# A two-pass graph network on one core: a fifth early group, row slots released by the reading product, half of the first stored unit summed between the passes

## The chip, the cores and the metric

The kernel runs on one core of one Trainium2 chip. The metric is device time in microseconds (us). Before the change it is 1505.38 us, the median of three runs (1504.96, 1505.38 and 1505.86). One further execution was recorded by the hardware profiler, and all rows below come from it.

## The reference

There are N = 6250 nodes with 96 features and E = 100000 edges, sorted by destination, each with 32 edge features and a weight. Two layers follow each other.

```
# layer 0: gated messages
e   = concat(x[src], edge_attr)
msg = (gelu(e @ mW1 + mb1) @ mW2 + mb2) * sigmoid(gelu(e @ gW1 + gb1) @ gW2 + gb2)
agg = segment_sum(msg, dst)
h   = layernorm(x + gelu(concat(x, agg) @ uW1 + ub1) @ uW2 + ub2) * ln_g + ln_b
x1  = layernorm(x + h)
# layer 1: graph convolution with self loops; deg and dinv come from the weights
out = segment_sum((x1 @ W)[src] * dinv[src] * weight * dinv[dst], dst) + self loop + b
x2  = layernorm(x1 + out)
```

## The kernel before, in words

Edges lie in 98 groups of 8 tiles of 128 edges, nodes in 49 blocks of 128. The kernel makes two passes over the groups.

**First pass** (layer 0). GpSimd (POOL) gathers the rows x[src] of each group with 8 indirect DMAs, TensorE (PE) transposes them and multiplies by the weights, ScalarE (ACT) applies gelu, VectorE (DVE) gates the messages, and PE sums them into windows of 72 nodes. Beside it, blocks of nodes that have all their messages are finished by `block1_sums` and `block1_rows` on DVE: the scaled node rows x1·dinv (`x_nat`, counted by the semaphore `s_xs`) go to a table in HBM, `x1s_table`.

**Second pass** (layer 1). It needs, for each edge, the scaled row of its source node. Half of the groups are *dense* (list `DENSE`, 48 of them): during the first pass a matrix of cells, one per group, was built and stored in HBM (`b_table`, 2 MB a unit). In the second pass SyncE (SP) loads a unit in two halves into one of three buffers, and PE multiplies it by all 49 blocks of `x_nat` (`dense_sums`, line 741). The other 50 groups are *gathered* (list `GATHERED`): POOL fetches their rows from `x1s_table`, 8 indirect DMAs a group, into one of 8 slots `rows`, DVE makes their one-hot matrix, and PE multiplies both (`gathered_sums`, line 823). Gathered groups are called G0 to G49 here, in the order in which POOL fetches them.

The second pass is written out in 26 *turns* (0 to 25). Turns 0, 1, 24 and 25 have one dense unit, the others two; `TAKES` says how many gathered groups each turn takes. Within a turn PE runs chunks 0 to 31 of the dense sum, with the turning over and placing of the turn before in between (`turn_over`, `place_sums`), then the gathered products, then output products of blocks that became whole (`outputs`, line 795), then chunks 32 to 48. DVE adds the sums of a turn into `acc1` after the next turn's `place_sums` (line 1444, semaphore `s_acc2`); the first gathered product of a turn waits for the additions of the turn before. Products in `ps_win` are counted by `s_win3`, in the order of PE.

**Between the passes.** PE finishes the last node blocks (`end1`, line 716), DVE normalises them in two batches of four (line 1343), PE transposes each batch (`turned_blocks`, line 766), ACT and SP write the rows to `x1s_table`. Four groups, 3, 5, 7 and 9, are *early* (`EARLY`, fetched first as G0 to G3): POOL fetches their rows from a second table, `x1s_early`, that holds the first 39 node blocks only (line 519), before `x1s_table` is whole. The part of those groups that comes from the last 10 blocks is computed on PE from cells made by DVE (`early_hots`) at the end of turns 1 and 3, two groups each: `early_cells` (line 834, 16 products a group that ACT copies out), `early_sums` (line 842), `early_placed` (line 851).

POOL reuses a row slot when the group eight places before it has been added to `acc1`:

```
if i >= SLOTS:
    pool.wait_ge(s_acc2, PLACE[GATHERED[i - SLOTS]] + 1)
```

Nothing is scheduled by the hardware or by a planner: each engine runs its own list, in the order written, and semaphores join them.

Of the kernel before, what the change touches and what calls it, by code (L numbers as in the profile page):

```python
# [5 lines left out]
P = 128  # L6
N, E = 6250, 100000
ND, ED = 96, 32
TG = 8
# [6 lines left out]
W = 72  # L16
# [13 lines left out]
TW = TG * WD  # L30
EARLY = (3, 5, 7, 9)
RUNS = ((0, 1), (10, 1), (12, 7), (20, 3), (24, 1), (26, 1), (28, 1), (30, 1), (32, 1), (34, 1), (36, 1),
        (39, 2), (42, 1), (44, 1), (46, 1), (48, 1), (50, 1), (52, 1), (54, 1), (57, 1), (59, 2), (62, 1),
        (64, 1), (66, 1), (68, 1), (70, 1), (72, 1), (74, 1), (76, 1), (78, 1), (80, 1), (82, 1), (86, 1),
        (88, 1), (90, 3), (94, 1))
DENSE = [g for first, n in RUNS for g in range(first, first + n)]
# [16 lines left out]
CELLS = 2 * HW  # L53
EARLY_IN = {1: (0, 1), 3: (2, 3)}
EARLY_TURN = list(EARLY_IN)
TAKES = (0, 1, 4) + 21 * (2,) + (1, 2)
HOTS = 6
# [35 lines left out]
assert len(DENSE) * TG == 2 * TWOS and sum(PAIRS) == len(DENSE) and not set(EARLY) & set(DENSE)  # L93
assert all(b - a == 2 for a, b in zip(EARLY, EARLY[1:]))
assert all(a + b <= HOTS for a, b in zip(TAKES, TAKES[1:]))
# [4 lines left out]
def gnn_kernel(nc, t, out):  # L100
# [11 lines left out]
    with ctx:  # L112
# [18 lines left out]
        win_off = sb("win_off", [P, NW])  # L131
        due_i = sb("due_i", [P, 1], i32)
        due = sb("due", [P, 1])
        mats = sb("mats", [P, HC + 5 * ND + 1])
# [14 lines left out]
        lo = sb("lo", [NG, 1])  # L149
        hi = sb("hi", [NG, 1])  # L150
        reach = sb("reach", [NG, 1])
        crossed = shared[0:NG, 4400:4400 + NW]
        extra = sb("extra", [NG, 1])
        spread = shared[0:NG, 2860:2860 + 3 * NG + 1]
# [14 lines left out]
        spare = x1b[:, :, :].rearrange("p b c -> p (b c)")  # L169
        win_i = spare[:, 5 * NT + 2 * NG + HC:5 * NT + 2 * NG + HC + NW].bitcast(i32)  # L170
        before, lo_all = [spare[:, 5 * NT + NG * i:5 * NT + NG * (i + 1)] for i in range(2)]
        b1_hi = spare[0:3, 5 * NT + 2 * NG:5 * NT + 2 * NG + HC].bitcast(bf16).rearrange("p (k c) -> p k c", k=2)
# [49 lines left out]
        hot_node = spare_g[:, 2 * ND:2 * (ND + W)].rearrange("p (m w) -> p m w", m=2)  # L222
        early_rows = spare_2[:, 0:NE * ND].rearrange("p (e c) -> p e c", e=NE)
        early_node = spare_c[:, 0:NE * W].rearrange("p (e w) -> p e w", e=NE)
# [291 lines left out]
        def _(pool):  # L516
# [50 lines left out]
            with pool.If(hard < 1):  # L567
                pool.wait_ge(s_zeroed, 16)
                pool.wait_ge(s_early, 16 * DONE_B)
                for i in range(NE):  # L570
                    pool.wait_ge(s_xt, NG - SLOTS + i + 1)
                    early_gathers(i)
                pool.wait_ge(s_xt, NG)
                pool.wait_ge(s_xsw, 16 * NB)
                for i, g in enumerate(GATHERED):
                    if i >= SLOTS:
                        pool.wait_ge(s_acc2, PLACE[GATHERED[i - SLOTS]] + 1)
                    if i == len(GATHERED) - 1:
# [12 lines left out]
        def _(pe):  # L591
# [139 lines left out]
            def dense_sums(q, chunks):  # L731
                if q == 0 and chunks[0] == 0:
                    pe.wait_ge(s_xs, NB - LAST)
                    pe.wait_ge(s_tile_out, TWOS)
                if chunks[0] == 0:
                    wait(pe, s_rowsumc, q - 1)
                for c in chunks:
                    if c % HH == 0:
                        for d in UNITS[q]:
                            pe.wait_ge(s_loaded[d % NU][c // HH], 16 * (d // NU + 1))  # L740
                    mm = nc.tensor.matmul(raw_sums(q), x_nat[:, c, :], stored_cells(q, c), start=(c == 0), stop=(c == NB - 1))  # L741
                    if c == HH - 1:
# [103 lines left out]
            def early_placed(q, es):  # L846
                pe.wait_ge(s_early_rows, early_part_of[es[0]] + 1)
                pe.wait_ge(s_early_node, 1)
                for m, e in enumerate(es):
                    col = len(TURNS2[q]) + m  # L850
                    nc.tensor.matmul(ps_win[0:ND, W * col:W * (col + 1)], early_rows[:, e, :], early_node[:, e, :],
                                     start=True, stop=True)
# [41 lines left out]
        def _(act):  # L894
# [116 lines left out]
            def early_part(es):  # L1011
                for e in es:
                    act.wait_ge(s_early_cells, 2 * e + 2)
                    wait(act, s_early_sums, e - 1)
                    for m in range(2):
# [4 lines left out]
                act.wait_ge(s_early_sums, es[-1] + 1)  # L1020
                nc.scalar.activation(early_rows[:, es[0]:es[-1] + 1, :],
                                     ps_hid[0][0:TW, 0:2 * ND].rearrange("p (e c) -> p e c", c=ND),
                                     ACT.Copy).then_inc(s_early_rows, 1)
# [14 lines left out]
        def _(dve):  # L1038
# [89 lines left out]
            dve.wait_ge(s_bcast8, 1)  # L1128
            of_early = lambda a: a[:, TG * EARLY[0]:TG * (EARLY[0] + 2 * NE)].rearrange("p (e s) -> p e s", s=2 * TG)[:, :, 0:TG]
# [11 lines left out]
            nc.vector.tensor_copy(src_early[:, :].rearrange("p (e k) -> p e k", k=TG), of_early(low8))  # L1141
# [3 lines left out]
            nc.vector.tensor_scalar(cell_early[:, :].rearrange("p (e k) -> p e k", k=TG),  # L1145
                                    of_early(cell[:, :, 0:1].rearrange("p t o -> p (t o)")), float(-DONE_B * WD), None, ALU.add).then_inc(s_bcast8, 1)

# [387 lines left out]
```

## Time and profile before

| | |
|---|---|
| median of three runs | 1505.38 us |
| profiled execution, its own time | 1507.1 us |
| span of its trace | 1505.3 us |
| mean granted TensorE clock | 0.984 |
| PE busy | 1397.7 us (93%) |
| DVE busy | 1087.5 us (72%) |
| POOL busy | 1119.1 us (74%) |
| ACT busy | 536.7 us (36%) |
| DMA | 283.06 MB, mean 188 GB/s |

Times in the rows are microseconds from the start of the span. The first pass ends at about 1008 us, turn 0 begins at about 1023 us. A row of the time sequence says when a group of instructions started, how long it lasted, how many there were (a float32 product is recorded as two), and in brackets how long the engine had been idle before it and what released it. Matmuls overlap a little, so from start to start is the better measure of what a group costs. POOL's busy time leaves out about 0.30 us of issue between two gathers.

### The profile page before, as it was taken

How to read it: one execution, taken by the hardware profiler on the slowest of the kernel's cores; microseconds unless marked ns; L12 is line 12 of the kernel's file. 1: busy time of each engine (PE TensorE's matmuls, PEld its weight loads, DVE VectorE, ACT ScalarE, POOL GpSimd, SP SyncE). 2: the span in 40 equal slices, each digit the busy share in tenths (PEclk: the TensorE clock that was granted, in tenths of full speed). 3: DMA queues.
4: the chain of work that ended last, by engine and by line, in shares of the span. 5: the costliest groups of instructions: out<-in, count | busy, mean ns of one | idle time of the engine just before them, and what ended most of it. 6: DMA issues, size and time to landing. Idle time of an engine off the chain costs nothing.

```text
span 1505.3 us, 27016 instructions
## 1 busy us (share of the span) xinstructions
PE 1397.7 (93%) x9260; PEld 1156.5 (77%) x9261; DVE 1087.5 (72%) x2883; ACT 536.7 (36%) x835; POOL 1119.1 (74%) x1192
## 2 busy tenths in 40 slices
PE   3899999999999999999999999987999999999887
PEld 2677777777777777777777677767999999998887
DVE  7688899989999988888899888867434343334234
ACT  1355555555555555555555555540000000000000
POOL 7777777777777777777777777775777777777774
PEclk9899999999999999999999999988999999999999
DMA  3455555555565556555655565557567877777772
GB/s 100 135 151 151 176 169 168 154 173 165 168 174 180 155 152 187 155 156 162 187 168 156 153 183 168 153 182 261 204 209 280 289 264 276 263 266 262 261 239 64
DMA packets 137992, 283.06 MB, mean 188 GB/s; under 512 B 53235, under 2 KB 102387, under 8 KB 137852
## 3 DMA queue, kind: packets, MB, share of 16 engines
q1 hardware_dynamic: 88860, 208.35, 38.3%
q0 software_dynamic: 37760, 58.07, 17.5%
q10 hardware_dynamic: 11232, 14.85, 3.4%
q8 instruction: 77, 1.26, 0.3%
q14 instruction: 63, 0.52, 0.1%
HBM read 176.08 MB, written 105.09 MB: 187 GB/s over the span
## 4 chain that ended last, share of the span: by engine, by line
PE 72%; POOL 7%; DMA 5%; DVE 4%; issue 4%; ACT 3%; DVEq 2%; SPq 0%; ACTq 0%
PE ps_hid L662 15%; PE ps_hid L685 11%; PE ps_xt L685 10%; PE ps_xt L741 10%; PE ps_win L605 9%; POOL rows L534 7%; PE ps_xt L632 5%; DMA large<-b_table 4%; PE ps_hid L659 4%; PE ps_win L823 3%; ACT large L913 3%; PE ps_bt L702 1%; DVE shared L1250 1%; PE ps_bn L716 1%; PE ps_bn L795 1%
## 5 line engine op out<-in xcount | busy, mean ns | idle before, releaser
L534 POOL DMA_INDIRECT rows<-in_x_nat,idx x782 | 741.5, 948 | 238.4 <-issue 238.0
L534 POOL DMA_INDIRECT rows<-x1s_table,idx x360 | 339.7, 944 | 118.5 <-issue 109.1
L741 PE MATMUL ps_xt<-large,x_nat 128*96 128x160 f32 (+1 forms) x2548 | 350.9, 293 | 12.8 <-DMA large<-b_table 12.8
L741 PEld LDWEIGHTS ps_xt<-large,x_nat 128*96 128x96 f32 x2548 | 333.5, 163 | 16.2 <-DMA large<-b_table 9.4
L662 PE MATMUL ps_hid<-mats,large 128*128 128x192 f32 x1568 | 321.2, 328 | 0.0
L662 PEld LDWEIGHTS ps_hid<-mats,large 128*128 128x128 f32 x1568 | 268.3, 191 | 44.2 <-issue 31.6
L913 ACT ACTIVATE large<-ps_hid 128x768 f32<-128x768 f32 x196 | 158.9, 811 | 165.2 <-PE ps_hid L662 165.2
L1250 DVE TENSOR_TENSOR shared<-cell,ps_fix 128x2000 f32<-128x2000 f32 x96 | 213.7, 2226 | 0.0
L685 PE MATMUL ps_hid<-shared 128*128 128x500 f32 x384 | 184.0, 601 | 22.5 <-ACT large L913 22.5
L685 PE MATMUL ps_xt<-shared 128*128 128x500 f32 x384 | 179.8, 591 | 6.0 <-DVE shared L1250 6.0
L953 ACT ACTIVATE shared<-ps_hid 128x1000 f32<-128x1000 f32 x96 | 96.4, 1005 | 198.3 <-PE ps_hid L685 198.3
L605 PEld LDWEIGHTS ps_win<-hot,large 128*98 128x98 f32 x1568 | 144.9, 167 | 18.3 <-issue 15.3
L605 PE MATMUL ps_win<-hot,large 128*98 128x72 f32 x1568 | 152.4, 250 | 5.5 <-DVE acc L1170 3.6
L1009 ACT ACTIVATE shared<-ps_xt 96x160 f32<-96x160 f32 (+1 forms) x26 | 7.5, 289 | 404.5 <-PE ps_xt L741 404.5
L659 PE MATMUL ps_hid<-b_split,ones_b 128*128 128x384 bf16 x392 | 128.8, 329 | 5.7 <-DVE step L1115 4.0
L1256 DVE TENSOR_SCALAR shared<-ps_fix,dst_i,weight 128x128 f32<-128x128 f32 x384 | 130.4, 401 | 2.0 <-PE ps_hid L685 2.0
L953 ACT ACTIVATE shared<-ps_xt 128x1000 f32<-128x1000 f32 x96 | 96.4, 1004 | 87.5 <-PE ps_xt L685 78.9
L685 PEld LDWEIGHTS ps_xt<-shared 128*128 128x128 f32 x384 | 69.8, 192 | 73.3 <-issue 67.0
L685 PEld LDWEIGHTS ps_hid<-shared 128*128 128x128 f32 x384 | 65.3, 190 | 76.9 <-issue 44.0
L632 PE MATMUL ps_xt<-ident,rows 128*96 128x128 f32 x784 | 103.5, 276 | 12.3 <-DMA rows<-in_x_nat,idx 6.7
L897 ACT ACTIVATE large<-ps_xt 96x1024 f32<-96x1024 f32 x98 | 99.9, 1019 | 36.0 <-PE ps_xt L632 30.3
L1444 DVE TENSOR_TENSOR acc<-acc,ps_win 96x72 f32 x97 | 21.9, 226 | 121.2 <-PE ps_win L810 105.9
(177 smaller groups left out, 1471.6 us busy)
## 6 DMA issues: line engine op xcount, KB each, us to landing
b_table<-shared SPq DMA_DIRECT2D x192, 500.0 KB
large<-b_table SPq DMA_DIRECT2D x96, 1000.0 KB, 5.2
rows<-in_x_nat,idx POOLq DMA_INDIRECT x782
large<-in_edge_t ACTq DMA_DIRECT2D x96, 128.0 KB
rows<-x1s_table,idx POOLq DMA_INDIRECT x366, 2.9
large<-in_x_t SPq DMA_DIRECT2D x7, 336.0 KB
x_nat<-in_x_nat SPq DMA_DIRECT2D x7, 336.0 KB
out_nodes<-shared SPq DMA_DIRECT2D x46, 48.0 KB
```

Source lines behind the costliest of these rows:

```text
L534: nc.gpsimd.indirect_dma_start(out=rows[slot][:, k, :], out_offset=None, in_=table, in_offset=bass.IndirectOffsetOnAxis(ap=idx[:, TG * g + ...
L605: mm = nc.tensor.matmul(ps_win[0:rws, 0:W], lhs[:, k, :], hot[u][:, k, :], start=(k == 0), stop=(k == TG - 1))
L632: mm = nc.tensor.transpose(ps_xt[m // 4][0:ND, P * (m % 4):P * (m % 4 + 1)], rows[v][:, m, :], ident[:, :])
L659: nc.tensor.matmul(ps_hid[j][:, 0:2 * HC], ones_b[:, :], flat(b1_split[:, :, :]), start=True, stop=False)
L662: mm = nc.tensor.matmul(ps_hid[j][:, HC * q:HC * (q + 1)], feat[u][:, P * m:P * (m + 1)], w1[:, :], start=False, stop=(q == 1))
L685: mm = nc.tensor.matmul(ps_pair[pair][:, m, 0:CELLS], ring_low[:, r, :], flat(ring_place[:, 2 * r:2 * r + 2, :]), start=True, stop=True)
L741: mm = nc.tensor.matmul(raw_sums(q), x_nat[:, c, :], stored_cells(q, c), start=(c == 0), stop=(c == NB - 1))
L897: nc.scalar.activation(feat[u][0:ND, :].rearrange("p (m c) -> p m c", m=2), ps_pair[0][0:ND, :, :], ACT.Copy).then_inc(s_feat, 1)
L913: nc.scalar.activation(flat(hid[u][:, 4 * half:4 * half + 4, :]).rearrange("p (j c) -> p j c", j=2), ps_pair[1][:, :, 0:2 * HC], ACT.Gelu) ...
L953: nc.scalar.activation(ready_b[i % READY].rearrange("p (h m x) -> p m h x", h=2, m=2), ps_pair[pair][:, :, 0:CELLS].rearrange("p m (h x) - ...
L1250: return nc.vector.tensor_tensor(place, cells.to_broadcast(shape), places_ps.rearrange("p (o w) -> p o w", o=1).to_broadcast(shape), ALU.i ...
L1256: nc.vector.tensor_scalar(low[:, i, :], places_ps[:, 0:P], src_low[:, t0 + k:t0 + k + 1], weight[:, t0 + k:t0 + k + 1], ALU.is_equal, ALU. ...
```

## The change

There are four edits.

1. `EARLY` gets a fifth group, 12, which was dense; group 27, which was gathered, becomes dense in its place. There are still 48 dense and 50 gathered groups. POOL fetches 40 instead of 32 times from `x1s_early`, and 358 instead of 366 times from `x1s_table`. The late part of the fifth group is computed alone, at the end of turn 5; its sum uses one of the two places of `early_rows` again.
2. POOL's wait before it reuses a slot is on `s_win3` (PE has read the rows) instead of `s_acc2` (DVE has added the sums).
3. The first 25 of the 49 chunks of turn 0 stand before the transposes of the last eight blocks instead of behind the first four of them.
4. Turn 2 takes three gathered groups instead of four, turn 23 one instead of two, turn 24 two instead of one, turn 25 three instead of two. All other turns take two as before, so from turn 3 to turn 22 each has used one group less than before.

Beside these, several small tiles move into shared memory, and twelve small DVE instructions come to the start of the program, since five early groups at uneven distance are copied one by one. Cut to what matters:

```
-EARLY = (3, 5, 7, 9)
+EARLY = (3, 5, 7, 9, 12)
-EARLY_IN = {1: (0, 1), 3: (2, 3)}
+EARLY_IN = {1: (0, 1), 3: (2, 3), 5: (4,)}
-TAKES = (0, 1, 4) + 21 * (2,) + (1, 2)
+TAKES = (0, 1, 3) + 20 * (2,) + (1, 2, 3)
...
-        early_rows = spare_2[:, 0:NE * ND].rearrange("p (e c) -> p e c", e=NE)
+        early_rows = spare_2[:, 0:2 * ND].rearrange("p (e c) -> p e c", e=2)
...
                     if i >= SLOTS:
-                        pool.wait_ge(s_acc2, PLACE[GATHERED[i - SLOTS]] + 1)
+                        pool.wait_ge(s_win3, PLACE[GATHERED[i - SLOTS]] + 1)
...
             def dense_sums(q, chunks):
                 if q == 0 and chunks[0] == 0:
-                    pe.wait_ge(s_xs, NB - LAST)
+                    pe.wait_ge(s_xs, HH)
                     pe.wait_ge(s_tile_out, TWOS)
...
                 upd_out(NB - 2, 2, *place(NB - 2))
+                dense_sums(0, range(0, HH))
                 turned_blocks(NB - 2 * LAST)
-                dense_sums(0, range(0, NB - LAST))
+                dense_sums(0, range(HH, NB - LAST))
                 turned_blocks(NB - LAST)
...
-            nc.vector.tensor_scalar(idx_early[:, :].rearrange("p (e k) -> p e k", k=TG), of_early(idx), DONE_B * P, None, ALU.min)
+            for e, g in enumerate(EARLY):
+                nc.vector.tensor_scalar(idx_early[:, TG * e:TG * (e + 1)], idx[:, TG * g:TG * (g + 1)], DONE_B * P, None, ALU.min)
```

The order on PE between the passes, before (716 the last node blocks, 766 the transposes of `turned_blocks`, 741 the chunks of turn 0):

```order
L716 MATMUL ps_bn<-mats,once 128x97
L766 MATMUL ps_bt<-ident,x_nat 96x128 [waits s_xs,s_xstc]
L766 MATMUL ps_bt<-ident,x_nat 96x128 x3
L741 MATMUL ps_xt<-large,x_nat 96x80 [waits s_loaded00,s_tile_out,s_xs]
L741 MATMUL ps_xt<-large,x_nat 96x80 x24
L741 MATMUL ps_xt<-large,x_nat 96x80 [waits s_loaded01]
L741 MATMUL ps_xt<-large,x_nat 96x80 x19
L766 MATMUL ps_bt<-ident,x_nat 96x128 [waits s_xs,s_xstc]
```

The same place of the changed kernel, whose lines are numbered two or three lower (713, 764, 738):

```order
L713 MATMUL ps_bn<-mats,once 128x97
L738 MATMUL ps_xt<-large,x_nat 96x80 [waits s_loaded00,s_tile_out,s_xs]
L738 MATMUL ps_xt<-large,x_nat 96x80 x24
L764 MATMUL ps_bt<-ident,x_nat 96x128 [waits s_xs,s_xstc]
L764 MATMUL ps_bt<-ident,x_nat 96x128 x3
L738 MATMUL ps_xt<-large,x_nat 96x80 [waits s_loaded01]
L738 MATMUL ps_xt<-large,x_nat 96x80 x19
L764 MATMUL ps_bt<-ident,x_nat 96x128 [waits s_xs,s_xstc]
```

The first 25 chunks have moved ahead of the first transposes; the other 20 stay between the two batches.

The order on PE at the end of turn 5 of the changed kernel (738 the last chunks of turn 5, 832 the cells of the fifth early group, 840 its sum over ten blocks, 849 its placing, the last 738 the first chunks of turn 6):

```order
L738 MATMUL ps_xt<-large,x_nat 96x160 x17
L832 MATMUL ps_hid<-shared 128x100 [waits s_early_hot,s_early_rows,s_early_out]
L832 MATMUL ps_hid<-shared 128x100 x3
L832 MATMUL ps_hid<-shared 128x100 [waits s_early_hot]
L832 MATMUL ps_hid<-shared 128x100 x3
L840 MATMUL ps_hid<-x_nat,shared 80x96 [waits s_early_out]
L840 MATMUL ps_hid<-x_nat,shared 80x96 x9
L849 MATMUL ps_win<-h_c,h 96x72 [waits s_early_node,s_early_rows]
L738 MATMUL ps_xt<-large,x_nat 96x160 [waits s_loaded10,s_loaded20,s_rowsumc]
```

Before, the chunks of turn 5 were followed by those of turn 6 at once; the seven rows between are new.

The order on POOL at the end of the early fetches, before (519 from `x1s_early`, 534 from `x1s_table`):

```order
L519 DMA rows<-x1s_early,idx_early 128x96 x7
L534 DMA rows<-x1s_table,idx 128x96 [waits s_xsw,s_xt]
L534 DMA rows<-x1s_table,idx 128x96 x31
L534 DMA rows<-x1s_table,idx 128x96 [waits s_acc2]
L534 DMA rows<-x1s_table,idx 128x96 x7
```

And of the changed kernel:

```order
L516 DMA rows<-x1s_early,idx_early 128x96 [waits s_xt]
L516 DMA rows<-x1s_early,idx_early 128x96 x7
L531 DMA rows<-x1s_table,idx 128x96 [waits s_xsw,s_xt]
L531 DMA rows<-x1s_table,idx 128x96 x23
L531 DMA rows<-x1s_table,idx 128x96 [waits s_win3]
L531 DMA rows<-x1s_table,idx 128x96 x7
```

Eight fetches have moved from behind the wait for the whole table (`s_xsw`) to ahead of it, and the slot waits name `s_win3`.

Since the fifth early group, 12, is whole only after turn 5, the first node blocks of the output become ready one turn later; the blocks 5 to 7 and 8 to 10, which had a turn each, both fall to turn 7 and stand behind each other there on PE. The blocks 41 to 43 go from turn 23 to turn 24.

## Rows read from the trace of the kernel before

**Rows 1.** Waits: who, released by whom: us in total, times, longest us

```profile
DVE ps_fix L1216 <- ACT squash L931: 52.9, 67, 6.8
...
PE ps_xt L741 <- DMA large<-b_table: 12.8, 13, 2.1
...
POOL rows L534 <- DMA x1s_table<-x_nat: 9.1, 1, 9.1
...
PE ps_win L823 <- DMA rows<-x1s_table,idx: 7.6, 4, 3.5
```

**Rows 2.** POOL in order of time: start, us, line, count [idle before]

```profile
1021.79 0.94 POOL L519 DMA_INDIRECT rows<-x1s_early,idx_early  x1 [0.30 <-issue]
1031.81 0.94 POOL L534 DMA_INDIRECT rows<-x1s_table,idx  x1 [9.07 <-DMA x1s_table<-x_nat]
...
1487.45 0.94 POOL L526 DMA_INDIRECT rows<-x1s_table,idx  x1 [0.30 <-issue]
```

**Rows 3.** PE in order of time, late in the second pass

```profile
1387.33 5.69 PE L741 MATMUL ps_xt<-large,x_nat 128*96 128x160 f32 x40
...
1401.40 1.50 PE L823 MATMUL ps_win<-dst_i,rows 128*96 128x72 f32 x16
1406.41 2.54 PE L823 MATMUL ps_win<-mats,rows 128*96 128x72 f32 x16 [3.52 <-DMA rows<-x1s_table,idx]
1408.75 6.42 PE L741 MATMUL ps_xt<-large,x_nat 128*96 128x160 f32 x40
...
1465.75 1.58 PE L823 MATMUL ps_win<-mats,rows 128*96 128x72 f32 x16 [2.48 <-DMA rows<-x1s_table,idx]
```

**Rows 4.** Three stretches, PE alone: length, busy us (count), granted clock, DMA share, GB/s

```profile
1024.00:1026.00 2.00, 2.00 (x15) 0.50 0.05 15
1028.00:1030.00 2.00, 2.00 (x27) 1.00 0.15 40
1407.00:1409.00 2.00, 2.00 (x14) 0.50 0.16 36
```

**Rows 5.** PE in order of time, around the early part of turn 3

```profile
1091.88 1.92 PE L834 MATMUL ps_hid<-shared 128*128 128x100 f32 x16
1094.79 2.03 PE L834 MATMUL ps_hid<-shared 128*128 128x100 f32 x16 [0.99 <-ACT shared L1018]
1097.81 3.53 PE L842 MATMUL ps_hid<-x_nat,shared 128*80 128x96 f32 x40 [0.99 <-ACT shared L1018]
1102.15 1.01 PE L741 MATMUL ps_xt<-large,x_nat 128*96 128x160 f32 x6
...
1145.19 2.18 PE L741 MATMUL ps_xt<-large,x_nat 128*96 128x160 f32 x14 [0.73 <-DMA large<-b_table]
```

**Rows 6.** PE in order of time, between the passes and in turn 1

```profile
1022.03 1.06 PE L766 MATMUL ps_bt<-ident,x_nat 128*96 128x128 f32 x4 [7.60 <-DVE x_nat L1343]
...
1032.88 0.60 PE L766 MATMUL ps_bt<-ident,x_nat 128*96 128x128 f32 x4
...
1040.19 1.55 PE L823 MATMUL ps_win<-hot,rows 128*96 128x72 f32 x16 [0.37 <-DVE acc L1444]
```

**Rows 7.** DVE in order of time, between the passes

```profile
1028.41 1.05 DVE L1343 TENSOR_SCALAR x_nat<-h_c,root,dinv 128x96 f32<-128x96 f32 x4
...
1039.81 0.23 DVE L1444 TENSOR_TENSOR acc<-acc,ps_win 96x72 f32 x1 [0.26 <-issue]
```

**Rows 8.** PE in order of time, the end

```profile
1488.42 0.62 PE L795 MATMUL ps_bn<-w_gcn,acc 96*128 96x96 f32 x4
...
1493.91 1.18 PE L823 MATMUL ps_hid<-hot,rows 128*96 128x72 f32 x12
1496.35 0.91 PE L795 MATMUL ps_bn<-w_gcn,acc 96*128 96x96 f32 x6 [1.25 <-DVE acc L1444]
```

**Rows 9.** DVE in order of time, the end

```profile
1495.25 0.23 DVE L1444 TENSOR_TENSOR acc<-acc,ps_win 96x72 f32 x1 [1.52 <-PE ps_hid L823]
...
1497.30 0.77 DVE L1460 SCALAR_TENSOR_TENSOR h<-ps_bn,dinv,x1b 128x96 f32<-128x96 f32 x3 [1.00 <-PE ps_bn L795]
```

More of the change, by code:

```diff
@@ L30 @@
 TW = TG * WD
-EARLY = (3, 5, 7, 9)
[L32 to L35, printed above, removed]
+EARLY = (3, 5, 7, 9, 12)
+RUNS = ((0, 1), (10, 1), (13, 6), (20, 3), (24, 1), (26, 3), (30, 1), (32, 1), (34, 1), (36, 1), (39, 2),
+        (42, 1), (44, 1), (46, 1), (48, 1), (50, 1), (52, 1), (54, 1), (57, 1), (59, 2), (62, 1), (64, 1),
+        (66, 1), (68, 1), (70, 1), (72, 1), (74, 1), (76, 1), (78, 1), (80, 1), (82, 1), (86, 1), (88, 1),
+        (90, 3), (94, 1))
 DENSE = [g for first, n in RUNS for g in range(first, first + n)]
@@ L93 @@
 assert len(DENSE) * TG == 2 * TWOS and sum(PAIRS) == len(DENSE) and not set(EARLY) & set(DENSE)
-assert all(b - a == 2 for a, b in zip(EARLY, EARLY[1:]))
 assert all(a + b <= HOTS for a, b in zip(TAKES, TAKES[1:]))
@@ L131, in gnn_kernel @@
         win_off = sb("win_off", [P, NW])
-        due_i = sb("due_i", [P, 1], i32)
-        due = sb("due", [P, 1])
         mats = sb("mats", [P, HC + 5 * ND + 1])
@@ L149, in gnn_kernel @@
         lo = sb("lo", [NG, 1])
-        hi = sb("hi", [NG, 1])
-        reach = sb("reach", [NG, 1])
+        hi, reach, extra = [shared[0:NG, 4514 + i:4515 + i] for i in range(3)]
         crossed = shared[0:NG, 4400:4400 + NW]
-        extra = sb("extra", [NG, 1])
         spread = shared[0:NG, 2860:2860 + 3 * NG + 1]
@@ L170, in gnn_kernel @@
         win_i = spare[:, 5 * NT + 2 * NG + HC:5 * NT + 2 * NG + HC + NW].bitcast(i32)
+        due_i = spare[:, 5 * NT + 2 * NG + HC + NW:5 * NT + 2 * NG + HC + NW + 1].bitcast(i32)
+        due = spare[:, 5 * NT + 2 * NG + HC + NW + 1:5 * NT + 2 * NG + HC + NW + 2]
         before, lo_all = [spare[:, 5 * NT + NG * i:5 * NT + NG * (i + 1)] for i in range(2)]
@@ L850, in early_placed @@
                     col = len(TURNS2[q]) + m
-                    nc.tensor.matmul(ps_win[0:ND, W * col:W * (col + 1)], early_rows[:, e, :], early_node[:, e, :],
+                    nc.tensor.matmul(ps_win[0:ND, W * col:W * (col + 1)], early_rows[:, e % 2, :], early_node[:, e, :],
                                      start=True, stop=True)
@@ L1020, in early_part @@
                 act.wait_ge(s_early_sums, es[-1] + 1)
-                nc.scalar.activation(early_rows[:, es[0]:es[-1] + 1, :],
-                                     ps_hid[0][0:TW, 0:2 * ND].rearrange("p (e c) -> p e c", c=ND),
+                nc.scalar.activation(early_rows[:, 0:len(es), :],
+                                     ps_hid[0][0:TW, 0:len(es) * ND].rearrange("p (e c) -> p e c", c=ND),
                                      ACT.Copy).then_inc(s_early_rows, 1)
@@ L1128, in _ @@
             dve.wait_ge(s_bcast8, 1)
-            of_early = lambda a: a[:, TG * EARLY[0]:TG * (EARLY[0] + 2 * NE)].rearrange("p (e s) -> p e s", s=2 * TG)[:, :, 0:TG]
             rel8, high8, low8 = [spare[:, NT * i:NT * (i + 1)] for i in range(3)]
@@ L1137, in _ @@
             nc.vector.tensor_scalar(low8, idx[:, :], P - 1, None, ALU.bitwise_and)
-            nc.vector.tensor_scalar(idx_early[:, :].rearrange("p (e k) -> p e k", k=TG), of_early(idx), DONE_B * P, None, ALU.min)
+            for e, g in enumerate(EARLY):
+                nc.vector.tensor_scalar(idx_early[:, TG * e:TG * (e + 1)], idx[:, TG * g:TG * (g + 1)], DONE_B * P, None, ALU.min)
             nc.vector.drain()
             nc.vector.tensor_copy(src_low, low8)
-            nc.vector.tensor_copy(src_early[:, :].rearrange("p (e k) -> p e k", k=TG), of_early(low8))
+            for e, g in enumerate(EARLY):
+                nc.vector.tensor_copy(src_early[:, TG * e:TG * (e + 1)], low8[:, TG * g:TG * (g + 1)])
             nc.vector.scalar_tensor_tensor(cell[:, :, 0:1], column(high8), float(WD), column(rel8), ALU.mult, ALU.add)
@@ L1144, in _ @@
             nc.vector.tensor_scalar(cell[:, :, 1:2], cell[:, :, 0:1], float(-HW), None, ALU.add)
-            nc.vector.tensor_scalar(cell_early[:, :].rearrange("p (e k) -> p e k", k=TG),
-                                    of_early(cell[:, :, 0:1].rearrange("p t o -> p (t o)")), float(-DONE_B * WD), None, ALU.add).then_inc(s_bcast8, 1)
+            for e, g in enumerate(EARLY):
+                last = nc.vector.tensor_scalar(column(cell_early[:, TG * e:TG * (e + 1)]), cell[:, TG * g:TG * (g + 1), 0:1],
+                                               float(-DONE_B * WD), None, ALU.add)
+            last.then_inc(s_bcast8, 1)
             def over_window(ap):
```

## The prediction

> **What bounds the kernel now.** I read the waits of the engines first, then PE, POOL and DVE in order of time over the second pass. POOL goes from gather to gather without a pause but one: it stands 9.07 us between the last fetch from `x1s_early` (started 1021.79) and the first from `x1s_table` (1031.81), which the landing of the table ends [rows 1, 2]. From there to the last gather at 1487.45 are 365 steps in 455.64 us, 1.248 us each, 9.99 us a group. No slot wait shows. PE is the other full engine. It waits in the second pass for three things: 13 times for halves of stored units, 12.8 us, and 4 times for gathered rows, 7.6 us [rows 1]; and for DVE between the passes [rows 6]. The four row waits lie late: from the last chunks of turn 19 to those of turn 20 PE takes 1408.75 − 1387.33 = 21.4 us, of which 3.5 are a row wait and 1.0 a slowed product [rows 3]; its own 17 us are less than the 20 that POOL needs for two groups, so the lead of the early rows is used up. The last of the four ends at 1465.75 [rows 3]; with 43 groups (G4 to G46) of 9.99 us from 1031.81, G46 was issued by 1461.4, so rows are usable about 4.3 us behind POOL's last gather of a group. From 1465.75 to the end no row is waited for: POOL's last group, issued by 1488.4, is usable by about 1492.7 and its product starts at 1493.91 [rows 2, 8]. So POOL sets the time until 1465.75, PE and DVE set the rest, and POOL's end lies only 1.2 us below.
>
> **The change part by part.**
>
> *POOL.* The fifth early group is 8 gathers, 9.99 us, from 1022.7, where POOL stood idle until 1031.81. It ends at about 1032.7, 0.9 us behind the landing. From then on group Gi is fetched 9.1 us earlier than before (i ≥ 5); G49 is issued by about 1479.8, usable by 1484.
>
> *Demand.* By `TAKES`, from turn 3 to 22 each turn uses one group less than before, at turn 23 two less. Together a group is wanted one group later and comes 9.1 us earlier: about 19 us of lead that PE does not have now, against row waits of 7.6 us in all. G44, the only one of turn 23, is usable by 1432.3 + 4.3 = 1436.6; before, that turn's second product ran at 1465.75 [rows 3], and even 15 us sooner it would find its rows there. So I take all four row waits away: −7.6 us. With them goes what followed the longest. After 3.52 us without work the granted clock stood at 0.50, that is 1.2 GHz, in 1407 to 1409; the product took 2.54 us instead of 1.50, the 40 behind it 6.42 instead of 5.69 [rows 3, 4]: −1.0 −0.7 = −1.7 us. Sum −9.3. No other wait for rows comes in their place as long as POOL isn't held by slots.
>
> *Slots.* POOL 9.1 us further ahead would want slots sooner. By the old rule G4's slot, product in turn 3, would come free only after the additions of turn 3, behind the placing in turn 4; by the new one as soon as PE is through with it, about a turn before. With 8 slots and POOL three to four groups ahead of PE I see no slot wait: 0. If this cover were gone, POOL has the 19 us to spend first.
>
> *The early part of turn 5.* It is new work on PE, with nothing beside it that PE could do. From the two groups of turn 3 [rows 5]: cells to the next start 1094.79 − 1091.88 = 2.9 us with the wait for ACT's copies; one of the two sums, half of 3.53 = 1.8; ACT's copy and placing, from the end of the sums (1101.3) to 1102.15, 0.8 for two, 0.7 for one. +5.4 us. It gives back the wait for the second half in turn 6, 0.73 us [rows 5], because the halves are loaded while PE does the early part, as there is no such wait in turn 4 behind the early part of turn 3. −0.7 us. The cells need DVE's `early_hots`, made a turn ahead, where DVE has idle time: 0.
>
> *Two parts in one turn.* In turn 7 PE computes blocks 5 to 7 and 8 to 10 behind each other in the same bank; the second waits until DVE has read the first. The nearest rows are those of the end: products from 1496.35, DVE reads from 1497.30 to 1498.07, so 1.7 us from the first product to the release, of which 0.7 is the products themselves [rows 8, 9]: +1.0 us, between 0 and 1.2.
>
> *The first half of turn 0.* Before, PE stood 7.60 us from 1014.43 to 1022.03 [rows 6]. The 25 chunks now run there. At the lower clock 15 products, 7.5 chunks, take 2.00 us; at the higher, 27 [rows 4]. So 25 chunks take at most 6.7 us and fit; if the load of unit 0 is late there are some 7 us until the second batch. Then 20 chunks at the higher clock, 3.0 us, and PE is at the second batch at about 1026, and waits there for DVE's last rows of `x_nat`, ready at 1029.46 [rows 7]. Before, it came at 1032.88. So PE is 3.4 us earlier; from there it needs 1039.82 − 1032.88 = 6.9 us to the gathered product of turn 1 and arrives at 1036.4. That product waits for DVE's addition of turn 0, started 1039.81 [rows 7], behind one-hot matrices that DVE makes one after another. DVE's path isn't touched, so PE starts again at 1040.2, as before: the stall has moved from one place to two, and the gain is 0. It can be 0.4 at best (the wait that DVE's addition already ends).
> What could make it a loss is the clock. PE now stands some 3.4 us at 1026 and up to 3.8 us before 1040. An idle of 3.52 us was followed by the lower clock, one of 2.48 us by a product of 1.58 us, so by none [rows 3]. If the first idle lowers the clock, the 6.9 us behind it grow and eat the second, and nothing is lost; if the second does, the loss is the 1.7 us above. I take 0, nearest to the first, since it comes first, and keep −0.4 to +1.7.
> The Trainium skill, TensorE: Matmul & The Clock Gate, section "Why this matters for your kernels", asks that PE have no long gaps between bursts, since an idle array falls back to half rate. It speaks against this edit, which splits one gap into two; by it the sum would be 1.7 us worse. The trace agrees at 1406 (0.50 behind 3.52 us) and can't show which of the two new gaps decides.
>
> *The end.* The third gathered product of turn 25 and the second of turn 24 are only moved from turns 2 and 23: PE's work is the same. DVE has one addition more in turn 25, 0.4 us (three take from 1495.25 to 1496.35 [rows 8, 9]), and one address more to fetch, beside 1.4 us more of PE work: between −0.4 and +0.4, taken 0.
>
> *The start.* Twelve small DVE instructions, under 0.2 us each by their neighbours, lie ahead of DVE's longest wait for ACT, 6.8 us [rows 1], in the first groups: 0. If that cover were gone, 2 us.
>
> **Sum.** −9.3 + 5.4 − 0.7 + 1.0 + 0 + 0 = −3.6 us. The profiled execution, 1507.1 us (span 1505.3), would become 1503.5. It lies 1.7 us above the median; against the median of 1505.38 that is 1501.8 us. PE, not POOL, sets the whole second pass then.
>
> **The rivals.**
>
> *Nothing to be told apart.* The moved stall lowers the clock before 1040 (+1.7 us), and the end costs 0.4 more: −1.5 us, 1503.9. For it: the length of the new idle. Against: the first idle comes before it.
>
> *Slower, by the stored units.* A PE that no longer waits for rows runs into the loads at every turn. The 13 waits are 1.0 us on average and 2.1 at the longest [rows 1]. If without the pauses of POOL each of them grew to 2.1, that is 13 × 1.1 = +14 us, so 1516; from 0.5 us more for each on it is slower than before (−3.6 + 6.5). For it: each wait comes from a load that is issued when the buffer is free, about as long before as PE needs to reach it. Against: most of these waits lie before the first row wait, where POOL wasn't in the way.
>
> *The half unit is worth what it frees.* If the addition of turn 0 comes sooner than DVE's rows say, the 3.4 us stay: −7.0 us, 1498.4. Against: DVE works without a gap up to 1039.81.
>
> *Rows are still waited for.* If a slot wait held POOL for long, or the fifth group's fetches delayed the table, part of the 7.6 us would stay: from −3.6 up to about +4, 1505.6 in the middle. Against: the lead of 19 us.
>
> **How the numbers follow.** A measurement of this kernel can tell about 0.2%, 3.0 us. Forecast 0.60, its own range 1499.8 to 1503.8, and in it a little over 3.0 us in three of five; nothing to tell apart 0.17; stored units 0.10; the half unit 0.07; rows 0.06. Faster by over 0.2%: 0.36 + 0.07 + 0.01 = 0.44. Within: 0.24 + 0.17 + 0.03 = 0.44. Slower: 0.10 + 0.02 = 0.12. The range takes in the half unit's gain in part and the first steps of the slower cases: 1498.3 to 1506.5.
>
> **What would show it.** Right: POOL without the 9 us gap at 1022, the first fetch from `x1s_table` at about 1032.7, its last at about 1479; no wait of PE for rows; PE idle at about 1026 and again before 1040, then the product of turn 1 at 1040.2; an early part of 5.4 us at the end of turn 5 and about 1 us of waiting in turn 7. Wrong: waits of PE for `large` of much more than 13 us, a product of turn 1 well before 1040, or POOL waiting on slots. If rows are waited for at all, the step on demand has failed.

## The result and the profile after

The change makes the kernel slower. Nine runs of the changed kernel have a median of 1514.62 us (1510.14 to 1519.19), nine of the kernel before 1505.86 us (1503.45 to 1509.01). The ratio is 1.0062, 95% interval 1.0046 to 1.0079: 9 us lost where 3.6 us less were forecast, and outside the range. One run of all those below, in the last experiment, was slow (2076.74 us at a granted clock of 0.654) and is left out of its median. The profiled execution took 1514.62 us, span 1512.7 us, mean granted clock 0.984 as before. Lines 456, 465, 738, 764, 793, 821, 832, 1344, 1445, 1461 and 1483 of the changed kernel are 459, 468, 741, 766, 795, 823, 834, 1343, 1444, 1460 and 1482 of the kernel before.

The waits of the changed kernel that answer to [rows 1] (who, released by whom: us in total, times, longest us):

```profile
PE ps_xt L738 <- DMA large<-b_table: 13.9, 11, 2.4
DVE shared L1483 <- DMA out_nodes<-shared: 6.7, 1, 6.7
PE ps_win L821 <- DVE acc L1445: 6.4, 2, 5.3
PE ps_bt L764 <- DVE x_nat L1344: 5.2, 2, 3.6
```

The four waits of PE for gathered rows, 7.6 us, are gone, as is POOL's 9.1 us. The waits for loads are 1.1 us more in all. New is the pair in the middle: DVE waits 6.7 us, once, for stores to `out_nodes`, and PE waits 5.3 us, once, for an addition of DVE.

POOL of the changed kernel in order of time, against [rows 2]:

```profile
1031.98 0.94 POOL L516 DMA_INDIRECT rows<-x1s_early,idx_early  x1 [0.30 <-issue]
1033.23 0.94 POOL L531 DMA_INDIRECT rows<-x1s_table,idx  x1 [0.30 <-issue]
...
1478.89 0.94 POOL L523 DMA_INDIRECT rows<-x1s_table,idx  x1 [0.30 <-issue]
```

The gap is filled and the last gather starts at 1478.89 instead of 1487.45, as forecast (1479). PE between the passes, against [rows 6]:

```profile
1021.75 0.61 PE L764 MATMUL ps_bt<-ident,x_nat 128*96 128x128 f32 x4 [1.60 <-DVE x_nat L1344]
1022.20 3.55 PE L738 MATMUL ps_xt<-large,x_nat 128*96 128x80 f32 x40
1029.30 1.06 PE L764 MATMUL ps_bt<-ident,x_nat 128*96 128x128 f32 x4 [3.56 <-DVE x_nat L1344]
1030.15 3.06 PE L738 MATMUL ps_xt<-large,x_nat 128*96 128x80 f32 x18
...
1039.88 1.55 PE L821 MATMUL ps_win<-hot,rows 128*96 128x72 f32 x16 [1.10 <-DVE acc L1445]
```

The chunks run in the first gap; PE stands at 1025.7 and again before 1039.88, and the product of turn 1 comes at 1039.88 as against 1040.19: the half unit moved the stall and gained nothing. The first new idle, 3.56 us, was followed by the lower clock (0.50 from 1030 to 1034), which ate the second down to 1.10 us. So both kernels begin the second pass alike, and the 7.4 us by which the span is longer lie behind this product: 465.1 us from it to the end before, 472.8 us now.

Where they lie is told by PE in turns 7 and 8 of the changed kernel (the turn that computes two output parts):

```profile
1167.50 3.76 PE L738 MATMUL ps_xt<-large,x_nat 128*96 128x160 f32 x14 [2.36 <-DMA large<-b_table]
1171.05 2.93 PE L821 MATMUL ps_win<-hot,rows 128*96 128x72 f32 x32
1173.82 0.85 PE L793 MATMUL ps_bn<-w_gcn,acc 96*128 96x96 f32 x6
1175.63 0.88 PE L793 MATMUL ps_bn<-w_gcn,acc 96*128 96x96 f32 x6 [0.95 <-DVE h L1461]
...
1195.87 2.81 PE L821 MATMUL ps_win<-prod,rows 128*96 128x72 f32 x16 [5.29 <-DVE acc L1445]
1198.47 2.77 PE L821 MATMUL ps_win<-dst_i,rows 128*96 128x72 f32 x16
1201.03 6.15 PE L738 MATMUL ps_xt<-large,x_nat 128*96 128x160 f32 x40
```

The 0.95 us at 1175 are the wait between the parts that the prediction priced. The 5.29 us before the products of turn 8 are not in it, and behind them PE runs slowly: 2.81, 2.77 and 6.15 us for what takes 1.50, 1.52 and 5.69 elsewhere [rows 3, 6], the granted clock being 0.50, 1.2 GHz, in this stretch:

```profile
1196.00:1201.00 5.00, 5.00 (x32) 0.50 0.98 403
```

The chain of waits of the changed kernel leads from this wait back through three engines (start, us, what; `...` stands for steps left out, which are issue times and single steps of DVE):

```profile
1181.24 0.32 SPq L456
...
1181.60 0.43 SPq L456
...
1182.08 0.43 SPq L465
...
1182.56 0.74 SPq L465
...
1183.35 8.28 DMA out_nodes<-shared
...
1191.66 0.60 DVE shared L1483 x3
...
1194.29 0.23 DVE acc L1445
...
1195.87 5.37 PE ps_win L821 x32
```

DVE normalises a part into the three places of the tile `y` (`shared` in the rows) and SP stores them. The second part of the turn, blocks 8 to 10, wants the same three places: `block2_norm` waits on `s_out` for the stores of blocks 5 to 7. Those stores were ready at 1180, but SP's list has them behind the wait for the end of the dense sum and the two loads of 1 MB that follow it (line 456, issued at 1181.24). They are issued from 1182.08 and land at 1191.63. Only then does DVE finish the part, fetch its addresses and make the additions of turn 7, for which PE waits. In the kernel before the parts lie a turn or more apart and the stores have a turn to land.

The Trainium skill, DMA: Bandwidth & Descriptors, section "Queues, rings and completion order", states that on each DMA engine the descriptors of one issuing engine's queue are consumed in the order of the ring. The trace agrees as far as it shows landings: three stores of 48 KB, issued 0.8 us behind 2 MB of loads on SP's queue, landed 8.28 us after the last of them was issued.

### The profile page after: what moved, and what is told of

Its sections match the earlier page's. It is cut to its first block, busy times and chain, and to the rows that moved or that the text cites. A ratio compares the mean times of both kernels' runs of the same rounds, so it can differ in the third digit from the quotient of the medians.

```text
span 1512.7 us, 27127 instructions
## 1 busy us (share of the span) xinstructions
PE 1405.2 (93%) x9298; PEld 1164.2 (77%) x9299; DVE 1093.4 (72%) x2907; ACT 537.9 (36%) x838; POOL 1119.3 (74%) x1192
## 3 DMA queue, kind: packets, MB, share of 16 engines
q0 software_dynamic: 37760, 58.07, 17.5%
## 4 chain that ended last, share of the span: by engine, by line
PE 76%; DMA 7%; DVE 6%; ACT 3%; DVEq 2%; issue 2%; SPq 0%; ACTq 0%
PE ps_xt L738 16%; PE ps_hid L659 15%; PE ps_hid L682 11%; PE ps_xt L682 10%; PE ps_win L602 8%; DMA large<-b_table 6%; PE ps_xt L629 5%; PE ps_win L821 4%; PE ps_hid L656 4%; ACT large L911 2%; DVE shared L1251 1%; PE ps_bn L793 1%; PE ps_bt L699 1%; PE ps_hid L832 1%; PE ps_bn L713 1%
## 5 line engine op out<-in xcount | busy, mean ns | idle before, releaser
L531 POOL DMA_INDIRECT rows<-x1s_table,idx x352 | 332.1, 944 | 107.3 <-issue 106.4
L738 PE MATMUL ps_xt<-large,x_nat 128*96 128x160 f32 (+1 forms) x2548 | 353.8, 295 | 14.4 <-DMA large<-b_table 13.9
```

Source lines behind the costliest of these rows:

```text
L531: nc.gpsimd.indirect_dma_start(out=rows[slot][:, k, :], out_offset=None, in_=table, in_offset=bass.IndirectOffsetOnAxis(ap=idx[:, TG * g + ...
```

## The experiments

Each was run with at least five timed runs beside the kernel before, and once with a profile; ratios are to the kernel before of the same batch. The expectations in microseconds were written for a kernel before at 1505 to 1507 us; its medians in the three batches were 1506.70 (the first four experiments), 1509.82 (the next four) and 1507.73 (the last two), so it is the ratios that are compared.

**The parts apart.** In `second_pass` of the changed kernel a part that becomes whole in the same turn as the one ahead of it is put into the next turn:

```
+    for i in range(1, len(parts)):
+        if parts[i][2] == parts[i - 1][2]:
+            parts[i] = (*parts[i][0:2], parts[i][2] + 1, parts[i][3])
```

> The changed kernel with one edit: the part of blocks 8 to 10 is handed to the turn after that of blocks 5 to 7, so that no turn computes two output parts. Theory A (the output stores): in turn 7 of the changed kernel the second part may only be written once the stores of the first part have landed, and SP issues these behind 2 MB of unit loads; DVE stood 6.71 us, PE then 5.29 us before the products of turn 8, and behind that the clock fell (2.81 and 2.77 us instead of 1.50 for two products, 6.15 instead of 5.7 for the chunks: 3.0 us), with 0.95 us between the two parts. Without it all of this goes: 9.2 us less than the changed kernel, about 1505.4 us, level with the kernel before (1503.5 to 1507). Theory B (the stored units): the changed kernel is slower because PE, free of row waits, waits longer for the loads in many turns; parting the two parts takes at most the 0.95 us away, 1512 to 1514 us, and the waits for the loads stay above 12 us in all.

Measured: 1508.55 us, ratio 1.0009 (0.9994 to 1.0024). DVE's wait for stores is gone, and with it 8 of the 9 us (1.0009 against 1.0062). The place was right. The time lies above the expected range all the same, 3 us over the 1505.4, and the waits for loads are longer, 15.5 us against 13.9:

```profile
PE ps_xt L741 <- DMA large<-b_table: 15.5, 11, 2.7
```

**The parts together, nothing else.** The kernel before, with blocks 5 to 7 put into the turn of blocks 8 to 10:

```
+    at = [part[0] for part in parts].index(5)
+    parts[at] = (*parts[at][0:2], parts[at + 1][2], parts[at + 1][3])
```

> The kernel before with one edit: the part of blocks 5 to 7 is held back by a turn, so that it falls into one turn with blocks 8 to 10, as in the changed kernel. Theory A: the profile shows the same stall, DVE 5 to 8 us for the output stores in turn 7 and PE 4 to 6 us before the products of turn 8; but here PE has row waits ahead (7.6 us and 1.7 us of slow clock) that a later PE no longer has, so the time moves only by 0 to +3 us: 1505.5 to 1509. Theory B: no wait of DVE for stores to speak of (under 2 us), time unchanged.

Measured: 1509.94 us, ratio 1.0016 (1.0003 to 1.0029). The same stall appears in a kernel that has nothing else of the change (DVE for the stores, then PE for DVE):

```profile
DVE shared L1484 <- DMA out_nodes<-shared: 6.5, 1, 6.5
PE ps_win L825 <- DVE acc L1446: 5.8, 2, 5.0
```

and the four waits for rows are gone: a PE that stands in turn 7 gives POOL the time that it took later. The stall costs about 2 us here (0.5 to 4.4 by the interval), not 8.

**The stores first.** In the changed kernel SP issues the stores of blocks 5 to 7 ahead of the wait for the dense sum and its loads, the parts staying together (`outputs` takes the part that begins with block 5 for `True`, the others for `False`):

```
+                    outputs(q - 1, (True,))
                     sp.wait_ge(s_rowsum, q + 1)
                     for d in UNITS[q]:
                         load(d + NU, 1)
-                    outputs(q - 1)
+                    outputs(q - 1, (False,))
```

> The changed kernel with SP issuing the three stores of blocks 5 to 7 before it waits for the end of turn 7's sum, so ahead of the two loads of second halves instead of behind them; both parts stay in turn 7. Theory A: DVE's wait for the stores falls from 6.7 to under 2 us, PE's wait before the products of turn 8 goes with it, the 0.95 us between the two parts stays: 8.3 us less than the changed kernel, about 1506.5 us (1504.5 to 1508). If it is having two parts in one turn and not the place of the stores in the queue, DVE still waits 4 us or more and the time stays above 1510. Theory B: above 1512.

Measured: 1508.65 us, ratio 1.0013 (0.9999 to 1.0028). DVE waits for no store. Issued ahead of the loads, the stores have landed by 1183.15, when DVE writes `y` again, so at most 4.0 us after the last of them was issued (SP, then DVE):

```profile
1177.86 1.29 SPq L465 DMA_DIRECT2D out_nodes<-shared  x3
1179.48 0.80 SPq L456 DMA_DIRECT2D large<-b_table  x2
...
1177.51 0.81 DVE L1484 TENSOR_SCALAR shared<-h,mv,root 128x96 f32<-128x96 f32 x3
...
1183.15 0.81 DVE L1484 TENSOR_SCALAR shared<-h,mv,root 128x96 f32<-128x96 f32 x3
```

PE's wait before the products of turn 8 is gone with it; in turns 7 and 8 are left the 0.95 us between the parts and a load wait of 1.86 us. So it is the place of the stores in SP's list, not the two parts as such.

**Without the half unit.** The changed kernel with the dense sum of turn 0 in one piece again, behind the first transposes:

```
-                dense_sums(0, range(0, HH))
                 turned_blocks(NB - 2 * LAST)
-                dense_sums(0, range(HH, NB - LAST))
+                dense_sums(0, range(0, NB - LAST))
```

> The changed kernel without its third edit: all 45 first chunks of turn 0 stand behind the first batch of transposes again. By the prediction's step the 3.4 us that PE gains there end at DVE's addition before 1040, so the time stays that of the changed kernel within 0.7 us. The rivals: the half unit is worth what it frees, +3.4 us without it; or the two new gaps lower the clock, -1.7 us without it.

Measured: 1515.48 us, ratio 1.0060 (1.0042 to 1.0078), as the changed kernel. The two intervals, each 5 us wide, would hardly rule out the rival's 3.4 us by themselves, but the traces do: from the last products of the node blocks (line 713) to the product of turn 1 are 26.96 us without the half unit, 26.70 with it and 26.90 in the kernel before. Without it:

```profile
1014.40 1.14 PE L713 MATMUL ps_bn<-mats,once 99*128 99x97 f32 x4 [0.62 <-ACT once L939]
...
1041.36 1.55 PE L820 MATMUL ps_win<-hot,rows 128*96 128x72 f32 x16 [0.80 <-DVE acc L1444]
```

The half unit is worth nothing here.

After these four the stall was settled, but a kernel without it was only level with before, where the other terms of the prediction's sum say 4.6 us less. What was left was load waits. In before they stand in two turns of three: at 1145, 1164, not in the next turn, at 1200, 1218, not in the next, and so on. This is the pattern of `UNITS`, which sorts a turn's pair by buffer and so puts it in reverse (3 before 2, 5 before 4, 9 before 8) in two turns of three. SP issues the loads in that order. Of the two units loaded behind a pair, the lower one is wanted in the next turn, the other a turn later.

**The loads in the order of the units.** The changed kernel with the parts apart, and

```
-                    for d in UNITS[q]:
+                    for d in sorted(UNITS[q]):
                         load(d + NU, 0)
                     sp.wait_ge(s_rowsum, q + 1)
-                    for d in UNITS[q]:
+                    for d in sorted(UNITS[q]):
                         load(d + NU, 1)
```

> The changed kernel with its two parts of turn 7 apart (as in the experiment that sets them apart), and SP issues the two loads of a half in the order of the units, not of their buffers. By the traces so far PE waits for a load in two turns of three: in those that follow a turn whose pair stands reversed (3 before 2, 5 before 4, 9 before 8), where the unit that PE wants next is loaded behind one that it wants a turn later. Theory A (the order makes the wait): load waits of PE fall from 15.5 us to under 4, the lower clock behind the longest goes with them; 1496 us (1494 to 1500), ratio to before 0.990 to 0.996. Theory B (the bytes make the wait, whichever load goes first): load waits stay at 13 to 16 us, 1508 (1506 to 1511).

Measured: 1499.41 us, ratio 0.9927 (0.9915 to 0.9940). PE waits for no load at all in the second pass, and its turns from turn 9 on take 17.5, 17.5 and 16.8 us in rotation. (The profiled execution, 1494.54 us, is the fastest of the five; the others took 1499.35 to 1499.52.) A turn of before and the same of this kernel; first before, PE in order of time:

```profile
1265.99 5.17 PE L741 MATMUL ps_xt<-large,x_nat 128*96 128x160 f32 x36
1272.43 2.15 PE L741 MATMUL ps_xt<-large,x_nat 128*96 128x160 f32 x14 [1.28 <-DMA large<-b_table]
```

then the kernel of this experiment:

```profile
1265.65 7.10 PE L741 MATMUL ps_xt<-large,x_nat 128*96 128x160 f32 x50
1272.59 2.60 PE L824 MATMUL ps_win<-hot,rows 128*96 128x72 f32 x29
```

The second halves are freed and loaded at the same point of the turn, with the same bytes; only the order differs. What PE waits for now is POOL, at the end:

```profile
PE ps_hid L824 <- DMA rows<-x1s_table,idx: 4.4, 2, 2.3
```

**The same order in the kernel before.** This kernel is the test of the prediction's first claim, that POOL sets the time of before until 1465.75.

> The kernel before, with the loads issued in the order of the units. Part of the claim of the prediction is that POOL sets the time of before until 1465.75 us. By that, PE gains nothing until there from shorter load waits: load waits fall from 12.8 us to under 4, row waits rise from 7.6 to some 16, only what lies after the last row wait and the clock change anything: 1505 (1503 to 1507), ratio 0.998 to 1.001. Rival: PE and its loads set the time there, POOL only in passing: 1496 (1494 to 1499). If the order doesn't matter: 1506.5, with the waits as they are.

Measured: 1510.38 us, ratio 1.0003 (0.9993 to 1.0012). The load waits, 12.8 us, are gone, and the time is the same, because PE runs into POOL:

```profile
PE ps_win L823 <- DMA rows<-x1s_table,idx: 16.6, 4, 5.0
```

against 7.6 us in [rows 1]. The last of these waits ends where POOL put it before:

```profile
1467.47 2.82 PE L823 MATMUL ps_win<-mats,rows 128*96 128x72 f32 x16 [1.87 <-DMA rows<-x1s_table,idx]
```

That is 434.7 us behind POOL's first fetch from `x1s_table`, against 433.9 us in the kernel before [rows 2, 3]. The rest of what PE gained it loses to the lower clock behind its row waits, 2.82 us for this product instead of 1.58. The claim holds. It also prices the change without its collision and without the load order in the way: from this kernel to the one above, 1.0003 to 0.9927, 11 us. These 11 us were not split among the four edits; the half unit showed nothing above, and the release is taken alone below.

**The old release of the row slots.** The changed kernel, parts apart, loads in the old order:

```
-                        pool.wait_ge(s_win3, PLACE[GATHERED[i - SLOTS]] + 1)
+                        pool.wait_ge(s_acc2, PLACE[GATHERED[i - SLOTS]] + 1)
```

> The changed kernel with the two parts apart, and POOL's row slots released by DVE's additions again, as before. The prediction put the slots at 0 because POOL, 3 to 4 groups ahead on 8 slots, does not meet them. By that: 1508.5 (1507 to 1510.5), ratio to before 0.999 to 1.003; slot waits of POOL in the late turns may show, of no consequence. Rival: with the longer lead POOL runs into its slots and the release by the product is what pays for it: row waits of PE come back in the late turns, 1510 to 1514.

Measured: 1510.30 us, ratio 1.0000 (0.9986 to 1.0013), not to be told from the new release. But with the old release POOL does meet its slots, early and not late, once for 4.7 us, until 1081:

```profile
POOL rows L534 <- DVE acc L1448: 5.0, 2, 4.7
```

**The addition of turn 0 first.** The parts apart, the loads in the order of the units, and DVE makes the addition of turn 0 between the one-hot matrices of the two early groups:

```
+                        if q == 0 and e == 0:
+                            node = first_node(turn[0])
...
+                            nc.vector.tensor_tensor(acc1[0:ND, ds(node, W)], acc1[0:ND, ds(node, W)],
+                                                    ps_win[0:ND, 0:W], ALU.add).then_inc(s_acc2, 1)
```

> As the kernel with the parts apart and the loads in the order of the units, and DVE makes the addition of turn 0 between the one-hot matrices of the first and the second early group, not behind both: its inputs are there at about 1035 us, so the product of turn 1 need not wait until 1040. PE arrives at 1038.8 in the changed kernel and waits 1.1 us (2.2 in the one with the parts apart). Theory A: that wait goes, 1 to 2 us less than the kernel with the unit order alone: 1494.5 (1492.5 to 1498.5). Rival: the later matrices of the second early group, 0.3 us, or a moved load wait eat it: equal to that kernel within 0.7 us.

Measured: 1499.17 us, ratio 0.9926 (0.9913 to 0.9939): no gain. PE has no wait before the product of turn 1 any more, but waits for rows instead, 4.2 us in turn 22 and 2.2 us at the end. The rival was right in the time; what ate the gain was POOL, which it did not name.

**The order of the loads alone.** The changed kernel, its parts together, with the edit of the loads.

> The changed kernel with the loads in the order of the units, its two parts still together in turn 7. The stall of turn 7 has nothing to do with the order of the loads, so DVE's wait for its own stores stays (5 to 7 us) and with it a PE wait of some 5 us and lower clock behind it, 7 to 8 us in all. With the parts apart and the loads in this order PE waits 4.4 us for rows at the end, behind POOL. Theory A (in that kernel POOL sets the end again): the stall is taken out of these 4.4 us first, so only 3 to 4 us reach the end: 1502.5 (1500.5 to 1504.5), and no row waits are left. Rival (the stall costs its full price wherever it lies): 1507 (1505.5 to 1508.5).

Measured: 1496.67 us, ratio 0.9923 (0.9905 to 0.9940). The stall is there in full, and no loss by it can be seen in the time (0.9923 against 0.9927 with the parts apart), less even than theory A allowed:

```profile
DVE shared L1483 <- DMA out_nodes<-shared: 6.6, 1, 6.6
PE ps_win L821 <- DVE acc L1445: 6.9, 2, 5.1
```

No wait for rows is left. From POOL's last gather to the end of the span are 15.9 us (1479.32 to 1495.2); with the parts apart they are 14.6 us (1478.22 to 1492.8). So in these two executions 1.3 us of a stall of some 9 reached the end. The profile with the parts apart also had lost 3.1 us in turn 1 to a low clock (below). Without that its row waits at the end would have been some 7.5 us, an estimate from the 4.4 and the 3.1; the expectation took the 4.4 us for the whole slack.

**The order of the loads with the old release.**

> The kernel with the parts apart and the loads in the order of the units, with POOL's row slots released by DVE's additions as in before. In the experiment with the old release and the old order of loads POOL stood 4.7 us in turn 2, at 1076 us, and that cost no time. Theory A (POOL sets the end here, so a stop of POOL is paid): POOL stands 3 to 5 us in turn 2, its last gather comes as much later, and the row waits of PE grow from 4.4 to some 8: 1503 (1501 to 1504.5). Rival (the stop finds cover as in the other kernel, or PE, faster now, frees the slots in time): 1499.4, equal to the kernel with the new release within 1 us.

Measured: 1498.94 us, the median of five runs, ratio 0.9939 (0.9918 to 0.9960). The trace is as theory A said:

```profile
POOL rows L534 <- DVE acc L1448: 4.1, 4, 3.2
PE ps_hid L824 <- DMA rows<-x1s_table,idx: 4.8, 2, 2.7
PE ps_win L824 <- DMA rows<-x1s_table,idx: 3.5, 1, 3.5
```

and POOL needs 448.5 us from its first fetch from `x1s_table` to its last instead of 445.7. The time decides nothing: it is 1.8 us longer by the ratios, between theory A's 3.6 us and the rival's 1 us, with an interval 6 us wide. The release by the product is worth at most a few microseconds here, and that is not shown in the time.

The three versions with the loads in the order of the units and the new release (parts apart, parts together, addition first) can't be told apart. They are 0.7 to 0.8% faster than the kernel before; the changed kernel is 0.6% slower than it.

## Why the prediction was wrong

**The step that failed** is "Two parts in one turn", taken at +1.0 us, between 0 and 1.2. The wait that it priced is there, 0.95 us. But the step followed PE's bank only, and not the next buffer of the same chain, the three places of `y`, whose release goes through SP's queue. Measured in its place, in the changed kernel: 0.95 us between the parts, 5.29 us before turn 8, and 2.9 us of lower clock behind (1.27 + 1.20 + 0.46, from start to start), together 9.2 us, 8.2 more than forecast. Its bounds were wrong too: both came from PE and DVE alone. The parts apart and the stores first, which take this one wait away in two ways, both give back 7 to 8 us; that is shown.

**What the other terms were.** The four row waits and the early part are as forecast. PE around the early part of turn 5, against [rows 5]:

```profile
1134.71 1.92 PE L832 MATMUL ps_hid<-shared 128*128 128x100 f32 x16
1137.62 1.88 PE L840 MATMUL ps_hid<-x_nat,shared 128*80 128x96 f32 x20 [0.99 <-ACT shared L1016]
...
1140.06 1.01 PE L738 MATMUL ps_xt<-large,x_nat 128*96 128x160 f32 x6
```

5.35 us against 5.4. The load wait of turn 6 is gone, but turn 7's grew from 0.91 to 2.36 us, and the 14 products behind it took 3.76 us instead of 2.14. So this term missed too: −0.7 us was forecast, and the loads cost 1.1 us more in waits and 1.6 us in lower clock. The half of turn 0 was 0, as taken, and of the two new idles the first lowered the clock, as argued; in another execution (last section) the second did so too, and cost 3.1 us, more than the 1.7 us that the prediction allowed it. The end: the third product of the last turn changed nothing; from the last gathered product to the end of the span are 11.2 us after and 11.4 before. Slots: 0, as taken; in the changed kernel no wait of POOL for a slot is longer than its usual 0.3 us. But a distance of three to four groups is not what keeps them away, for with the old release POOL stands 4.7 us.

The sum for the second pass of the changed kernel: 465.1 − 3.6 = 461.5 forecast; + 8.2 (turns 7 and 8) + 1.8 (load waits, 1.1 more instead of 0.7 less) + 1.6 (the clock behind that of turn 7) = 473.1, against 472.8 measured.

**The rivals.** None of the four is what happened. "Slower, by the stored units" gave the right sign for a wrong reason: load waits grew by 1.1 us, not 14. But it looked at the place where the next few microseconds lie.

**What stays open.** Without the collision the kernel is level with before, where the sum says 4.6 us less. In the profile with the parts apart the second pass takes 465.0 us, 4.5 more than the 465.1 − 4.6 = 460.5 of that sum. Load waits are 3.4 us of it (15.5 against 12.8 − 0.7), and lower clock behind one of them is 1.6 us: 5.0 us, so together they account for all of it. But the load waits of the profiles with the old load order are 12.8 and 13.7 us without the fifth early group and 13.9, 15.5, 14.7, 13.6 and 12.9 us with it: on average 0.9 us more, with a scatter as large. Whether the change itself made them longer is not shown. That they are the order of the loads is: in the new order they are 0, with the change and without it.

## What to carry to other kernels

When a change lets two passes through a buffer fall into one period, follow every buffer of that chain to what releases it, through the queue of the engine that does so: a ready store waits behind what that engine's list has ahead of it. A wait that comes in two periods of three has a cause with that rhythm; look for it before it is taken as the price of the bytes. And price a stall by what bounds the end: the same stall of some 9 us cost next to nothing where POOL set the end, and 7 to 8 us where PE did.

## What the runs showed of the hardware

The length of an idle of PE alone does not say whether the lower clock follows. Of idles in the second pass, 1.93 us (parts apart, at 1335) was followed by 14 products in 3.79 us and a granted clock of 0.54, but 2.13 us of the same execution (at 1170) by 14 products in 2.15 us and a clock of 1.00, and 2.71 us (at 1374) by 14 products in 2.18 us and a clock of 1.00 again; 2.48 us in before was not followed by it [rows 3]. The three rows of the kernel with the parts apart:

```profile
1169.90 2.15 PE L741 MATMUL ps_xt<-large,x_nat 128*96 128x160 f32 x14 [2.13 <-DMA large<-b_table]
...
1335.18 3.79 PE L741 MATMUL ps_xt<-large,x_nat 128*96 128x160 f32 x14 [1.93 <-DMA large<-b_table]
...
1373.99 2.18 PE L741 MATMUL ps_xt<-large,x_nat 128*96 128x160 f32 x14 [2.71 <-DMA large<-b_table]
```

In the kernel with the loads in the order of the units, an idle of 2.00 us before the product of turn 1 cost more than itself: the product took 2.81 us instead of 1.55, the 34 behind it 4.91 instead of 3.06, and turn 1 26.8 us instead of 23.7.

```profile
1039.59 2.81 PE L824 MATMUL ps_win<-hot,rows 128*96 128x72 f32 x16 [2.00 <-DVE acc L1448]
1042.19 4.91 PE L741 MATMUL ps_xt<-large,x_nat 128*96 128x80 f32 x34
```

The granted clock stood at 0.50 from 1040 to 1046. Before the same product, idles of 2.21 us (parts apart, loads in the old order) and 1.87 us (parts together, loads in the order of the units) were followed by the usual 1.55 us.

The Trainium skill, TensorE: Matmul & The Clock Gate, section "Why this matters for your kernels", warns of long gaps between bursts of products. These idles are shorter than the 3.52 us on which the prediction weighed it, so here short ones could cost the clock too, though not each time.
